# GRU blocks on one Trainium2 core: variance plus eps and minus mean move from GpSimd to VectorE, behind the merge of the statistics

## The reference

```python
def _mingru(x, Wz, bz, Wh, bh):
    z = sigmoid(einsum('bsi,hi->bsh', x, Wz) + bz)
    h_tilde = tanh(einsum('bsi,hi->bsh', x, Wh) + bh)
    a = clip(1.0 - z, CLAMP_LO, CLAMP_HI)
    return _linear_scan(a, z * h_tilde)          # along the sequence

def _layernorm(x, gamma, beta):
    mu = mean(x, axis=-1, keepdims=True)
    var = mean(square(x - mu), axis=-1, keepdims=True)
    return (x - mu) * rsqrt(var + LN_EPS) * gamma + beta

for i in range(L):                               # L = 4, for each direction
    h_new = _mingru(h, Wz[i], bz[i], Wh[i], bh[i])
    if i > 0:
        h_new = h_new + h
    h = _layernorm(h_new, gamma, beta)
```

## Time and profile before

| what | us |
| --- | --- |
| median of 3 runs | 1570.84 (1570.65 to 1571.08) |
| the profiled execution, its own time | 1570.97 |
| its span, first to last instruction | 1569.1 |
| PE busy in it | 1528.1 (97%) |
| DVE busy | 1347.7 (86%) |
| ACT busy | 1029.0 (66%) |
| POOL busy | 1034.5 (66%) |

### The profile page before, as it was taken

One profiled execution on the slowest core, in us unless ns is written; L12 is line 12 of the kernel. 1 busy time (PEld: TensorE's weight loads), 2 busy tenths in 40 slices (PEclk: granted clock), 3 DMA queues, 4 the chain that ended last, 5 costly groups with the idle time before them and its releaser, 6 DMA issues.

```text
span 1569.1 us, 22973 instructions
## 1 busy us (share of the span) xinstructions
PE 1528.1 (97%) x7690; PEld 1258.0 (80%) x7690; DVE 1347.7 (86%) x1915; ACT 1029.0 (66%) x1689; POOL 1034.5 (66%) x1271
## 2 busy tenths in 40 slices
PE   5999999999999999999999999999999999999999
PEld 3777887878888878888788878888888888888887
DVE  5998889998999989899988878788888878787877
ACT  4888978889778799687897634444444444544454
POOL 2776666767868678877778745556556656555566
PEclk9999999999999999999999999999999999999999
DMA  4021131412312111311224371020202011110101
GB/s 168 8 81 68 34 121 48 141 62 75 129 53 82 41 54 41 115 61 48 102 75 168 128 242 53 8 88 21 88 21 88 20 61 48 59 49 27 41 14 41
DMA packets 72865, 112.66 MB, mean 72 GB/s; under 512 B 5159, under 2 KB 37927, under 8 KB 69678
## 3 DMA queue, kind: packets, MB, share of 16 engines
q1 hardware_dynamic: 72750, 111.21, 20.9%
HBM read 73.43 MB, written 37.76 MB: 71 GB/s over the span
## 4 chain that ended last, share of the span: by engine, by line
PE 70%; DVE 5%; ACT 4%; issue 1%; ACTq 0%; DVEq 0%
PE ps L498 22%; PE ps L583 15%; PE ps L602 14%; PE ps L552 11%; PE ps L518 3%; PE ps L532 3%; ACT H L831 1%; DVE bnp L1103 1%; ACT AH L835 1%; PE ps L565 1%; DVE H L1092 1%; DVE H L1091 1%; ACT ps L795 1%; DVE AL L1115 1%; ACT yb L794 1%
## 5 line engine op out<-in xcount | busy, mean ns | idle before, releaser
L498 PE MATMUL ps<-AH,WH 128*128 128x512 f32 x896 | 368.2, 411 | 7.8 <-DVE H L1092 6.1
L498 PE MATMUL ps<-AL,WH 128*128 128x512 f32 x896 | 351.6, 392 | 0.0
L498 PE MATMUL ps<-AH,WL 128*128 128x512 f32 x896 | 350.5, 391 | 0.0
L1650 POOL TENSOR_TENSOR acq<-acq,sq 128x512 f32<-128x512 f32 x120 | 181.8, 1515 | 152.0 <-ACT sq L926 151.4
L1527 POOL TENSOR_TENSOR H<-H,yb 128x512 f32<-128x512 f32 x192 | 250.7, 1306 | 32.1 <-DVE yb L1083 26.2
L1083 DVE TENSOR_TENSOR_SCAN yb<-ab,ps 128x512 f32<-128x512 f32 x192 | 232.5, 1211 | 9.8 <-POOL ab L1518 1.5
L913 ACT ACTIVATE g<-ps 128x512 f32<-128x512 f32 x128 | 76.5, 597 | 249.6 <-PE ps L583 249.6
L794 ACT ACTIVATE yb<-ps,ncnd 128x512 f32<-128x512 f32 x224 | 156.2, 697 | 124.9 <-PE ps L498 121.5
L1518 POOL TENSOR_SCALAR ab<-yb 128x512 f32<-128x512 f32 x224 | 139.9, 625 | 122.1 <-ACT yb L794 110.7
L1278 DVE SCALAR_TENSOR_TENSOR gl<-g,wcol,gh 128x512 fp32r<-128x512 f32 x118 | 133.7, 1133 | 93.4 <-ACT gh L923 93.4
L498 PEld LDWEIGHTS ps<-AH,WH 128*128 128x128 f32 x896 | 169.0, 189 | 44.7 <-DVE H L1092 9.5
(11 more groups left out here) (172 smaller groups left out, 3309.5 us busy)
## 6 DMA issues: line engine op xcount, KB each, us to landing
hs_scratch<-H SPq DMA_DIRECT2D x16, 1024.0 KB, 5.5
hc<-hs_scratch SPq DMA_DIRECT2D x32, 512.0 KB, 4.4
xr<-in_x SPq DMA_DIRECT2D x32, 256.0 KB, 4.5
out<-ob SPq DMA_DIRECT2D x32, 256.0 KB, 2.2
xbuf<-in_x SPq DMA_DIRECT2D x7, 1024.0 KB, 7.9
RAW<-in_wt SPq DMA_DIRECT2D x16, 256.0 KB, 6.9
stg<-in_fct SPq DMA_DIRECT2D x16, 256.0 KB, 3.2
stg<-in_pjt SPq DMA_DIRECT2D x16, 256.0 KB, 2.9
```

What stands on the lines that cost most here:

```text
L498: r = e.matmul(GATE[i % 3][:], w[:, q, m * 128:(m + 1) * 128], a[:, q, :], start=(n == 0), stop=(n == 11))
L1650: e.tensor_tensor(acq[b % 2][:], acq[b % 2][:], sq[:], ALU.add).then_inc(f_s2, 1)
```

## The change

GpSimd no longer makes `vep` and `nmp`. VectorE makes both at the end of `stats`, from `mvp` in SBUF. It first waits until its own two merges are complete. `inv` waits for `vep` and makes only the power and the product. The buffers, the eight slots of the ring of statistics and the order of all other work stay as they are. `SHIFT_S` numbers the `nmp` in the order of `stats`. The input's own statistics (`inv_x`) stay on GpSimd.

```diff
@@ numbering
+SHIFT_S = {u: n + 1 for n, u in enumerate(u for u in STATS if layer(u) < 3)}
@@ VectorE, stats(tau, pr)
             for i in range(2):
                 e.wait_ge(s_bs, 2 * n + i + 1)
                 e.bn_aggr(mvp[:, r, i, :], bnp[:, r, i, :]).then_inc(s_ag, 1)
+            e.wait_ge(s_ag, 2 * n + 2)
+            e.tensor_scalar(vep[:, r, :], mvp[:, r, :, 1], EPS, None, ALU.add).then_inc(s_ve, 1)
+            if TAILS[tau][2] < 3:
+                e.tensor_scalar(nmp[:, r, :], mvp[:, r, :, 0], -1.0, None, ALU.mult).then_inc(s_nm, 1)
@@ GpSimd, inv(tau, pr)
-            e.wait_ge(s_ag, 2 * STATS[p])
-            e.tensor_scalar(vep[:, r, :], mvp[:, r, :, 1], 1.0, EPS, ALU.mult, ALU.add).then_inc(s_ve, 1)
-            if l < 3:
-                e.tensor_scalar(nmp[:, r, :], mvp[:, r, :, 0], -1.0, 1.0, ALU.mult, ALU.mult).then_inc(s_nm, 1)
-            e.wait_ge(s_ve, INVS[p])
+            e.wait_ge(s_ve, STATS[p])
             if l == 3:
                 e.tensor_tensor(rl[:, b, d, 2 * pr:2 * pr + 2], vep[:, r, :], nhalf[:, 0:2], ALU.pow).then_inc(s_rs, 1)
                 return
             e.tensor_tensor(rsp[:, r, :], vep[:, r, :], nhalf[:, 0:2], ALU.pow).then_inc(s_rs, 1)
-            e.wait_ge(s_nm, SHIFTS[p])
+            e.wait_ge(s_nm, SHIFT_S[p])
             e.wait_ge(s_rs, INVS[p])
             e.tensor_tensor(nbp[:, r, :], nmp[:, r, :], rsp[:, r, :], ALU.mult).then_inc(s_nb, 1)
```

## The result

| kernel | median us (lowest to highest) |
| --- | --- |
| before | 1570.87 (1570.65 to 1571.08) |
| after | 1586.24 (1586.04 to 1586.76) |

The ratio is 1.0099, with a 95% interval of 1.0086 to 1.0111. The changed kernel is slower by 15.4 us, or 1%. The forecast was 1593 with a range of 1577 to 1599, so the sign and the mechanism held, and the size was 7 us too large.

A forecast was written before the change was run, and what follows sets the result against it. TensorE was taken as the bound, with VectorE close behind. 1570.97 us plus 7.4 to 10.1 for issue, 13.2 to 14.4 for holding and 0 for GpSimd gave 1591.6 to 1595.5, taken as 1593, range 1577 to 1599.

The forecast's parts named there:

- What bounds the kernel: GRU stage: TensorE is the bound, busy 759.05 of 775 us, VectorE close behind at 703.00; TensorE waits for VectorE.
- GpSimd's relief at 0: GpSimd gives up 42.8 us of busy time and the power starts earlier, but ScalarE's order covers it: 0 us.
- Rival 3: Shorter chain through GpSimd wins at ScalarE's 23 waits for `nbp`, gaining 5.5 us: 1565.5 us; chance 0.07.
- Issue cost: VectorE's `stats`: issuing the pair delays its next work; 7.4 to 10.1 us were to reach the path.
- Rival 2: VectorE's delays fall into slack, within 3 us of no change: 1571 to 1574 us; chance 0.08.
- The new instructions are held: VectorE's `vep` and `nmp` on SBUF last until a running GpSimd instruction ends; chance 0.62, 1593 us.
- rival 1: The stride of two keeps `vep` and `nmp` from being held, leaving only issue cost: 1578 to 1581 us; chance 0.23.
- The size of holding: VectorE waiting for GpSimd: about 47 instructions held for 22 us, of which 13.2 to 14.4 reach TensorE.
- TensorE's wait at the earlier trace: TensorE's wait for the scan near 749.40 us was to grow from 0.90 to about 1.5 us.
- The stall at the earlier trace: TensorE's slot near 829.37 us was to show 0.53 us of stall where there was none.
- VectorE's busy time: In the GRU stage it was to grow by 50 us or more, or 30 to 35 without holding.

The follow-up runs named there:

- e3: The kernel before with `vep` and `nmp` left out on every engine, so normalised values differ: 1569.93 us.
- e1: The kernel before with two more merges (one in the last layer) on VectorE into an unread spare tile, after a wait for its own merges: 1579.57 us.
- e6: The kernel before plus the change's two VectorE `tensor_scalar` into an unread spare tile, on one element a partition instead of two: 1580.09 us.
- e9: The kernel before with only VectorE's wait for its own two merges added at the end of each `stats` call: 1575.75 us.
- e2: The kernel before plus the change's two VectorE `tensor_scalar` into an unread spare tile, while GpSimd keeps its own `vep` and `nmp`: 1585.93 us.
- e7: The kernel before plus two unused VectorE `tensor_tensor` with two SBUF inputs, `mvp` and a constant tile, into a spare tile: 1586.96 us.

## Why the prediction was right, and its size was not

- **What bounds the kernel.** TensorE, with VectorE close behind and small margins: right. Places without a margin at the scan went from 12 to 39, and TensorE's longer waits are for VectorE.
- **GpSimd's relief at 0.** Right to about 1.2 us (e3). The chain to the power did get 0.21 us shorter, and ScalarE's order covers it, as forecast. Rival 3 (faster) fails on this.
- **Issue cost, 0.25 to 0.30 us a call.** It measured 0.265. On the path, 7.4 to 10.1 us were forecast. e1, with a slightly dearer pair, gave 8.4, and e6, with a slightly cheaper one, 8.8. This term is right. Rival 2 (slack) needed it to vanish, and e9 shows that even 0.12 us a call is felt.
- **The new instructions are held.** Right, and rival 1 fails: a stride of two doesn't prevent it. The Trainium skill's rule on its page "VectorE: DVE Perf Modes", section "Mode 2×_2P" ("outermost non-unit dim even (or odd and equal for src and dst)", with no word on the stride), agrees with e2. An instruction on one element has no such dimension, so the sentence doesn't settle it. e6 does: 0 of 224 were held. Its page "SBUF — State Buffer", section "Who interferes with whom", says that an instruction with two SBUF inputs contends with a GpSimd instruction that reads SBUF, and e7 agrees.
- **The size of holding is the step that failed.** 47 held instructions with 22 us were forecast, of which 13.2 to 14.4 on the path. There were 31 with 12.3 us, of which e2 against e1 puts 6.4 on the path. Three reasons can be read. How much each of them makes of the difference was not separated. First, the price of one encounter. The forecast took all that was left of GpSimd's instruction (0.56 us at the earlier trace rows) as extra, on top of the issue cost, although a small instruction takes 0.17 us of that time anyway. Counted in the forecast's way the 31 have 16.4 us. The slot of the earlier trace rows shows it. The first line is from the kernel before, the others are its counterparts after the change:

```profile
824.20 1.26 DVE L1115 TENSOR_TENSOR AL<-ps,AH 128x512 fp32r<-128x512 f32 x2
```
```profile
838.10 0.30 DVE L1108 BATCH_NORM_AGGREGATE mvp<-bnp 128x2 f32<-128x6 f32 x2
...
839.00 1.28 DVE L1121 TENSOR_TENSOR AL<-ps,AH 128x512 fp32r<-128x512 f32 x2
...
840.80 1.28 DVE L1105 BATCH_NORM_STATS2 bnp<-ps 128x6 f32<-128x512 f32 x2
...
842.48 1.21 DVE L1085 TENSOR_TENSOR_SCAN yb<-ab,ps 128x512 f32<-128x512 f32 x1
...
843.30 0.39 PE L500 MATMUL ps<-AL,WH 128*128 128x512 f32 x1
...
843.75 0.50 PE L500 MATMUL ps<-AH,WH 128*128 128x512 f32 x1
```

Again 0.56 us of `keep` is left when `vep` starts (838.44 to 839.00). But `low` starts 0.90 us after the first merge instead of 0.22, so the call costs 0.68 us: 0.26 for issue and 0.42 for holding, where the forecast had 0.30 + 0.56. Of this the wait for the second `bn_stats` takes up 0.40 (1.80 us from `low` to it instead of 2.20), not the 0.34 that the row gives as idle time, because back-to-back instructions overlap. The second call adds 0.26. The scan thus ends 0.54 us later, and the matmul starts 0.45 us after the one before it instead of 0.23: a stall of 0.22 us where 0.53 was forecast.

Second, the forecast took each call's phase from the trace before. It had GpSimd in `keep` at the merge's end in 33 calls and in `add` in 15. After the change `vep` starts inside a `keep` in 16 calls and inside an `add` in 15. In ten of the 33, `keep` had started only 0.05 us before `vep` would, as in the earlier trace rows, so a shift of a few hundredths lets the pair through. Third, I let `nmp` be caught by the `keep` behind an `add`. That never happened: after an `add`, `nmp` or the next work started before `keep` did. And the earlier trace rows, shown for it, was a call of the last layer (line 1541 follows in GpSimd's queue), which has no `nmp` at all. After the change that place reads:

```profile
416.86 1.29 POOL L1533 TENSOR_TENSOR H<-H,yb 128x512 f32<-128x512 f32 x1
...
417.11 1.06 DVE L1110 TENSOR_SCALAR vep<-mvp 128x2 f32<-128x2 f32 x1
418.09 1.27 DVE L1121 TENSOR_TENSOR AL<-ps,AH 128x512 fp32r<-128x512 f32 x2
...
418.23 0.61 POOL L1524 TENSOR_SCALAR ab<-yb 128x512 f32<-128x512 f32 x1
```

The eight long `nmp` are of another kind. There, `vep` got in 0.01 to 0.05 us before `keep`, and `nmp`, 0.08 us behind `vep`, did not:

```profile
222.59 0.17 DVE L1110 TENSOR_SCALAR vep<-mvp 128x2 f32<-128x2 f32 x1
222.60 0.63 POOL L1524 TENSOR_SCALAR ab<-yb 128x512 f32<-128x512 f32 x1
222.67 0.59 DVE L1112 TENSOR_SCALAR nmp<-mvp 128x2 f32<-128x2 f32 x1
```

- **The sum by the runs:** 8.4 for issue (e1), 6.4 for holding (e2 less e1), and 0.6 left over of 15.4. The 0.6 is the distance between e2 and the changed kernel, each against the kernel before, and is well within their intervals.
- **Signs named beforehand.** TensorE's wait at the earlier trace rows was to grow to about 1.5 us and grew to 1.68. The stall at the earlier trace rows appeared, with less than half of the forecast size. VectorE's busy time grew by 36.6 us over the span (1384.3 against 1347.7), less than the 50 that I named. Most of the shortfall is holding. The issue part was too high as well: the pages of e6 and e1 show 25.2 and 27.7 us more busy time without holding, where I had 30 to 35, since the wait for the merges is idle time.

## What to carry to other kernels

An average load of 91% says little; look at each place where the bound engine starts as soon as another one has finished, and count what a new instruction puts ahead of it. Small VectorE instructions on SBUF between GpSimd instructions have a second price that their usual duration doesn't show: find rows of the same kind in the trace that overlap a GpSimd instruction, and read the maximum and not the mean. If a result is needed only by an idle engine, issue it one instruction later than its input is ready, so that the wait for the own engine's result is free. Here the version with both pairs issued later took 1575.6 instead of 1586.2 us, though how much of that is the wait was not measured. And if possible don't move it at all.

## What the runs showed of the hardware

- A VectorE `tensor_scalar` on two elements a partition in SBUF, normally 0.17 us, lasts until a running GpSimd instruction ends: up to 1.06 us during a 128x512 addition. The same with a `tensor_tensor` of two SBUF inputs (1.07 us). One element a partition (0.15 us) and merges (0.15 to 0.18 us) are not held, with 51 and 53 encounters.
- One or two hundredths of a microsecond decide an encounter. A `vep` that started 0.01 us before `keep` took 0.17 us, and an `nmp` that started 0.015 us behind one (near 823.8 us) took 0.16. In e7 an instruction 0.01 us behind `keep` was held for 0.62, and after the change a `vep` 0.05 us behind it (838.44 and 838.39) took 0.59.
- A wait of VectorE for its own last small instruction costs 0.12 us each time, even with nothing behind it that needs the result; 128 of them cost this kernel 4.7 us.
- GpSimd's durations for `add` and `keep` hardly changed (means of 1298 and 633 ns after, 1306 and 625 before).
